# Perceiver layer on one core: the key stack's transfers on three queues and in the attention's block, routing in fewer and wider steps, own rows gathered tile by tile

## The reference, cut to what matters

```
x = x + cross_attention(layernorm(x), ctx)
Q, K, V = split(h @ WQ.T), split(h @ WK.T), split(h @ WV.T)     # h = layernorm(x)
Q, K = layernorm(Q), layernorm(K)                               # per head
context = softmax(Q @ K.T / sqrt(32)) @ V
z = context @ mean(sparse_W_V); z = z where z is among its head's 128 largest, else 0
x = x + (z * mean(sparse_W_O)) @ WO.T
probs = softmax(h2 @ Wg)                                        # h2 = layernorm(x), 8 experts
top_vals, top_idx = top_k(probs, 2); top_vals /= sum(top_vals)
x = x + sum over e of scores[e] * (relu(h2 @ W1[e] + b1[e]) @ W2[e] + b2[e])
```

## Time and profile before

| | us |
|---|---|
| median of 3 runs | 1640.94 (1640.29 to 1644.56) |
| the profiled execution | 1640.97 |
| its span, first to last instruction | 1639.3 |
| TensorE busy | 1523.3 |
| VectorE busy | 1265.9 |
| ScalarE busy | 1012.3 |
| GpSimd busy | 416.9 |

### The profile page before, as it was taken

The page is one execution under the profiler, slowest core; times in us unless marked ns, Lnnn a source line. Parts: engine busy times, 40 slices in busy tenths (PEclk is TensorE's granted clock), DMA queues, the critical chain, the costliest instruction groups (busy, mean ns, idle before and its releaser), DMA issues. The chain is left out here.

```text
span 1639.3 us, 22322 instructions
## 1 busy us (share of the span) xinstructions
PE 1523.3 (93%) x8112; PEld 836.7 (51%) x8112; DVE 1265.9 (77%) x1909; ACT 1012.3 (62%) x1241; POOL 416.9 (25%) x219
## 2 busy tenths in 40 slices
PE   6799999999999989999999999999877964799998
PEld 4466666666665433333333333333334421699996
DVE  5677676776777879999999999999665758477664
ACT  3366666666666678888888888888243530144441
POOL 5445545636545013204002100100104140100002
PEclk9899999999999989999999999999897986799999
DMA  4454444453534564456554445444342026289994
GB/s 171 162 190 145 167 168 149 160 180 129 193 142 142 140 156 126 112 150 187 126 143 114 123 110 128 115 117 103 52 99 56 1 97 269 72 308 355 365 351 135
DMA packets 119836, 254.50 MB, mean 155 GB/s; under 512 B 10152, under 2 KB 26536, under 8 KB 115248
## 3 DMA queue, kind: packets, MB, share of 16 engines
q1 hardware_dynamic: 118016, 248.88, 48.7%
q0 software_dynamic: 1280, 4.20, 0.8%
q10 hardware_dynamic: 432, 0.01, 0.0%
HBM read 182.26 MB, written 61.34 MB: 149 GB/s over the span
## 5 line engine op out<-in xcount | busy, mean ns | idle before, releaser
L748 ACT ACTIVATE att_pr<-att_sc 128x1024 f32<-128x1024 f32 x512 | 496.2, 1022 | 74.4 <-PE att_sc L665 74.4
L798 DVE TENSOR_TENSOR att_tot<-att_tot,att_pr 128x2048 f32<-128x2048 f32 x200 | 467.2, 2336 | 21.1 <-ACT att_pr L748 0.9
L491 DVE CUSTOM_DVE_ANT_0 ctx_size<-ctx_tot,ctx_size 128x512 f32<-128x512 f32 x512 | 333.1, 689 | 136.2 <-PE ctx_tot L411 132.1
L462 ACT ACTIVATE ctx_size<-ctx_dif 128x1024 f32<-128x1024 f32 x256 | 262.3, 1025 | 125.5 <-PE ctx_dif L411 125.4
L665 PE MATMUL att_sc<-g_stacks,att_kst 98*128 98x512 f32 x1024 | 308.8, 424 | 1.5 <-DVE g_stacks L589 1.5
L665 PEld LDWEIGHTS att_sc<-g_stacks,att_kst 98*128 98x128 f32 x1024 | 173.6, 189 | 236.1 <-ACT att_pr L748 210.8
L679 PE MATMUL att_o<-att_pr,att_val 128*32 128x512 f32 x2048 | 272.9, 605 | 2.0 <-issue 1.9
L411 PE MATMUL ctx_dif<-ctx_k_dif,f_q_hi 32*128 32x512 f32 x512 | 128.8, 500 | 8.9 <-DVE ctx_best L491 4.9
L411 PE MATMUL ctx_tot<-ctx_k_sum,f_q_hi 32*128 32x512 f32 x512 | 129.0, 500 | 0.0
L86 PE MATMUL f_proj<-f_wv_hi,g_stacks 128*128 128x512 f32 x320 | 121.1, 421 | 0.0
L86 PE MATMUL f_proj<-g_stacks,f_wk_hi 128*128 128x512 f32 x352 | 120.4, 424 | 0.0
(11 more groups left out here) (287 smaller groups left out, 2095.4 us busy)
## 6 DMA issues: line engine op xcount, KB each, us to landing
m_w<-in_W SPq DMA_DIRECT2D x30, 2048.0 KB, 10.6
att_kst<-keys_scratch SPq DMA_DIRECT2D x192, 256.0 KB, 3.9
f_raw<-in_ctx SPq DMA_DIRECT2D x32, 1024.0 KB, 6.0
keys_scratch<-f_k_hi SPq DMA_DIRECT2D x32, 512.0 KB, 2.8
keys_scratch<-f_k_lo SPq DMA_DIRECT2D x32, 512.0 KB, 3.2
values_scratch<-ctx_v SPq DMA_DIRECT2D x32, 512.0 KB, 3.1
att_val<-values_scratch SPq DMA_DIRECT2D x64, 256.0 KB, 2.7
rows_scratch<-mix_blank SPq DMA_DIRECT2D x1, 3840.0 KB, 23.7
```

Source lines behind the costliest of these rows:

```text
L462: act.activation(size[:, i % ABS, :], dif[:, :], ACT.Abs).then_inc(s_size, 1)
L491: dve.tensor_tensor_reduce(out=size[:, i % ABS, r * CH:(r + 1) * CH], in0=tot[i % 2][:, r * CH:(r + 1) * CH], in1=size[:, i % ABS, r * CH: ...
L748: act.activation(pr[:, T % SLOTS, 2 * s:2 * s + 2, :], sc[(2 * T + s) % PAIRS][:, :].rearrange("p (j q) -> p j q", j=2), ACT.Exp, scale=SC ...
L798: dve.tensor_tensor(tot[b % 2][:, :, :], so_far, pr[:, T % SLOTS, :, :], ALU.add).then_inc(s_add, 1)
```

## The change

**Key stack.** `key_rows` becomes a function that takes the issuing engine. In `self_projections` SyncE issues the high band at place 0 for group 0, ScalarE the one at place 2 (ahead of its last value copy), and GpSimd the low band (after `s_lo` has reached 8, with a semaphore of its own, `c.s_copy[2]`). The bands of groups 1 to 3 are issued by SyncE as its only work in `self_attend`. TensorE waits there for `c.s_copy[0]` and `c.s_copy[2]` before step 0, and for `c.s_copy[1]` before step 16 as before.

```diff
+def key_rows(engine, c, part, place, groups, done):
+    for j in range(HG):
+        src, dst = part[HD * j:HD * j + HD, groups, :], c.skst[HD * place:HD * place + HD, j::HG, :][:, groups, :]
+        engine.dma_start(f32(dst), src).then_inc(done, 16)
...
-            for groups, done in ((slice(0, 1), c.s_copy[0]), (slice(1, G), c.s_copy[1])):
-                sp.wait_ge(s_hi, TILES)
-                key_rows(f32(hi[1][:, :, :]), 0, groups, done)
-                key_rows(f32(hi[1][:, :, :]), 2, groups, done)
-                sp.wait_ge(s_lo, TILES)
-                key_rows(f32(lo[1]), 1, groups, done)
+            sp.wait_ge(s_hi, TILES)
+            key_rows(sp, c, f32(hi[1][:, :, :]), 0, slice(0, 1), c.s_copy[0])
...
             affine(TILES - 1)
+            act.wait_ge(s_hi, TILES)
+            key_rows(act, c, f32(hi[1][:, :, :]), 2, slice(0, 1), c.s_copy[0])
...
             pool.wait_ge(s_ones, 1)
+            pool.wait_ge(s_lo, TILES)
+            key_rows(pool, c, f32(lo[1]), 1, slice(0, 1), c.s_copy[2])
...
+        @block.sync
+        def _(sp):
+            for part, place in ((f32(c.own_hi[1][:, :, :]), 0), (f32(c.own_hi[1][:, :, :]), 2), (f32(c.own_lo[1]), 1)):
+                key_rows(sp, c, part, place, slice(1, G), c.s_copy[1])
...
-            pe.wait_ge(c.s_copy[0], 16 * HG * 6)
+            pe.wait_ge(c.s_copy[0], 16 * HG * 5)
+            pe.wait_ge(c.s_copy[2], 16 * HG)
```

```diff
-            for t in range(NT):
-                pe.matmul(count, every[:, :], mask[:, t, :], start=(t == 0), stop=(t == NT - 1)).then_inc(s_rank, 1)
-            for t in range(NT):
-                for u in range(t):
-                    pe.matmul(rank[:, t, :], every[:, :], mask[:, u, :], start=(u == 0), stop=False)
-                mm = pe.matmul(rank[:, t, :], earlier[:, :], mask[:, t, :], start=(t == 0), stop=True)
-            mm.then_inc(s_rank, 1)
+            for u in range(NT):
+                pe.matmul(rank[:, u + 1:, :], every[:, :], mask[:, 0:NT - u, :],
+                               start=(u == 0), stop=False, skip_group_check=True)
+            pe.matmul(rank[:, 0:NT, :], earlier[:, :], mask[:, :, :],
+                      start=False, stop=True, skip_group_check=True).then_inc(s_rank, 1)
...
+            tops = [go(dve.max(out=top[:, t, :], in_=prob[:, t, :])) for t in range(NT)]
             for t in range(NT):
-                step(dve.max(out=top[:, t, :], in_=prob[:, t, :]))
-                step(dve.max_index(out=idx[:, t, :], in_max=top[:, t, :], in_values=prob[:, t, :]))
...
+                dve.wait_ge(s_step, tops[t])
+                indexed = go(dve.max_index(out=idx[:, t, :], in_max=top[:, t, :], in_values=prob[:, t, :]))
+            summed = go(dve.tensor_tensor(two[:, :], top[:, :, 0], top[:, :, 1], ALU.add))
+            dve.wait_ge(s_step, indexed)
+            cast = go(dve.tensor_copy(idf[:, :, :], idx[:, :, :]))
+            dve.wait_ge(s_step, summed)
+            inverted = go(dve.reciprocal(rt[:, :], two[:, :]))
+            dve.wait_ge(s_set, 8)
+            dve.wait_ge(s_step, cast)
+            step(dve.tensor_tensor(pick[:, :, :, :], both(tall(iota[:, :])),
+                                   pairs(idf).unsqueeze(3).broadcast_to([P, 2, NT, E]), ALU.is_equal))
...
+            step(dve.tensor_tensor(more[:, :, :], count.unsqueeze(1).broadcast_to([P, 3, E]), edges[:, :, :], ALU.is_gt))
+            reached = go(dve.tensor_tensor(reach[:, :, :, :], more[:, :, :].unsqueeze(1).broadcast_to([P, E, 3, E]),
+                                           below[:, :, :, :], ALU.mult))
+            tiles = go(dve.tensor_reduce(extra[:, :], more[:, :, :].rearrange("p k e -> p e k"), AX.X, ALU.add))
+            dve.wait_ge(s_step, reached)
+            led = go(dve.tensor_reduce(ahead[:, :], reach[:, :, :, :].rearrange("p e k f -> p e (k f)"), AX.X, ALU.add))
...
+            step(dve.tensor_tensor(spots[:, :, :, :], pick[:, :, :, :], both(place[:, :, :]), ALU.mult))
+            step(dve.tensor_reduce(c.where[:, :, :], spots[:, :, :, :], AX.X, ALU.add))
+            dve.tensor_copy(c.slot[:, :].rearrange("p (k t) -> p k t", k=2), c.where[:, :, :]).then_inc(s_slot, 1)
```

```diff
+        OWN = (3, 5, 7, 8)
...
-                pe.wait_ge(s_own, 2 * NT)
-                for k in range(DC):
-                    for t in range(NT):
+                biases(range(0, NT // 2))
+                for t in range(NT):
+                    pe.wait_ge(s_own, OWN[t])
+                    for k in range(DC):
                         mm = pe.matmul(tx[:, k, :], c.h[:, t, k * P:(k + 1) * P], own[:, t, :],
-                                       start=(t == 0), stop=(t == NT - 1))
+                                       start=(t == k == 0), stop=(t == NT - 1), skip_group_check=True)
                 mm.then_inc(s_tx, 1)
...
+                biases(range(NT // 2, NT))
```

More of the change, by code:

```diff
@@ L937, in _ @@
         def _(sp):
-            def key_rows(part, place, groups, done):
-                for j in range(HG):
-                    src, dst = part[HD * j:HD * j + HD, groups, :], c.skst[HD * place:HD * place + HD, j::HG, :][:, groups, :]
-                    sp.dma_start(f32(dst), src).then_inc(done, 16)
             sp.wait_ge(s_hi, NT)
@@ L1369, in mix_and_route @@
         idf = sb("idf", [P, NT, 8])
-        pick = [sb(f"pick{k}", [P, NT, E]) for k in range(2)]
+        pick = sb("pick", [P, 2, NT, E])
         mask = sb("mask", [P, NT, E])
@@ L1374, in mix_and_route @@
         rt = sb("rt", [P, NT])
-        more = [sb(f"more{k}", [P, E]) for k in range(3)]
-        upto = [sb(f"upto{k}", [P, E]) for k in range(2)]
+        more = sb("more", [P, 3, E])
+        extra = sb("extra", [P, E])
+        reach = sb("reach", [P, E, 3, E])
+        ahead = sb("ahead", [P, E])
         move = sb("move", [P, E])
@@ L1621, in _ @@
-            step(dve.tensor_tensor(place[:, :, :], rank[:, :, :], late[:, :, :], ALU.add))
-            step(dve.scalar_tensor_tensor(out=place[:, :, :], in0=tall(iota[:, :]), scalar=128.0, in1=place[:, :, :],
-                                          op0=ALU.mult, op1=ALU.add))
-            for k in range(2):
-                step(dve.tensor_tensor(mine[:, :, :], pick[k][:, :, :], place[:, :, :], ALU.mult))
-                step(dve.tensor_reduce(c.where[:, k, :], mine[:, :, :], AX.X, ALU.add))
-                dve.tensor_copy(c.slot[:, NT * k:NT * k + NT], c.where[:, k, :]).then_inc(s_slot, 1)
@@ new lines, in _ @@
+            placed = go(dve.scalar_tensor_tensor(out=place[:, :, :], in0=tall(iota[:, :]), scalar=128.0, in1=rank[:, 0:NT, :],
+                                                 op0=ALU.mult, op1=ALU.add))
+            dve.wait_ge(s_step, led)
+            moved = go(dve.scalar_tensor_tensor(out=move[:, :], in0=ahead[:, :], scalar=128.0, in1=shifted[:, :],
+                                                op0=ALU.mult, op1=ALU.add))
+            dve.wait_ge(s_step, tiles)
+            go(dve.tensor_tensor(c.upto[:, :], ahead[:, :], extra[:, :], ALU.add))
@@ new lines, in _ @@
+            dve.wait_ge(s_step, moved)
+            step(dve.scalar_tensor_tensor(out=late[:, :, :], in0=rank[:, 0:NT, :], scalar=128.0, in1=tall(move[:, :]),
+                                          op0=ALU.is_ge, op1=ALU.mult))
+            dve.wait_ge(s_step, placed)
+            step(dve.tensor_tensor(place[:, :, :], place[:, :, :], late[:, :, :], ALU.add))
+            step(dve.tensor_tensor(spots[:, :, :, :], pick[:, :, :, :], both(place[:, :, :]), ALU.mult))
+            step(dve.tensor_reduce(c.where[:, :, :], spots[:, :, :, :], AX.X, ALU.add))
@@ L1645, in _ @@
                       allow_small_or_imprecise_dtypes=True).then_inc(s_set, 1)
-            pool.wait_ge(s_set, 4)
+            pool.wait_ge(s_set, 6)
+            pool.affine_select(out=below[:, :, :, :].rearrange("p e k f -> p e (k f)"),
+                               in_=every[:, 0:3 * E].unsqueeze(1).broadcast_to([P, E, 3 * E]),
+                               compare_op=ALU.is_gt, fill=0.0, base=0, pattern=[[1, E], [0, 3], [-1, E]],
+                               channel_multiplier=0).then_inc(s_set, 1)
             pool.affine_select(out=earlier[:, :], in_=every[:, :], compare_op=ALU.is_gt, fill=0.0,
@@ L2010, in perceiver_layer @@
                 c.own_lo = [c.own_pr[:, n, :, :] for n in range(2)]
-                c.s_copy = [sem(f"copy{n}") for n in range(2)]
+                c.s_copy = [sem(f"copy{n}") for n in range(3)]
                 self_projections(nc, c)
```

108 lines of the change are left out of this document (55 added, 53 removed).

## The result

The kernel after took 1628.51 us (median of 4 runs, 1626.45 to 1632.10), the kernel before 1642.15 beside it (1640.29 to 1644.56): ratio 0.9918, 95% interval 0.9895 to 0.9941, so 13 us gained, 10 to 17. The forecast was 1624.9. The profiled execution of after is its longest, 1632.10 (span 1630.4), against 1640.97 of before: 8.9 us less.

What follows compares the result with a forecast made beforehand. TensorE, 93% busy, was taken as the bound on average, idling at the key stack and routing. Parts of 9.0, 5.0 and 2.1 sum to 16.1: 1640.97 to 1624.9 us; own range 1622 to 1628, with rivals 1 and 2 1620 to 1632.

Steps and rivals of the forecast that it cites:

- What bounds the kernel: Whole kernel: TensorE bounds on average, 93% busy; an 18.2 us gap without compute and the routing's VectorE chain delay it.
- Part A: Key stack: issues spread over three engines, groups 1 to 3 moved; TensorE restarts at 1228.5 instead of 1237.55, 9.0 us gained.
- The barrier's own term: Between projections and attention: TensorE's first product follows the last issue by 0.94 us, so 1227.6, before the landing at 1228.5.
- Rivals 1 and 4: GpSimd's key transfers: 1, dear at 2.2 us each, 1628.7, chance 0.18; 4, they hold the core, 1646 at 6.5, chance 0.03.
- rival 3: Attention: starts early but is held at product 17 by the transfers of groups 1 to 3; about 1641, chance 0.03.
- Same cost as now: Attention's restart: the clock falls in the shorter gap and rises some 4 us after work begins, as before; no loss taken.
- rival 2: Clock pattern differs: low stretch at 1256 to 1262 goes (1622) or costs (1628), or biases don't lift it (1626.6); chance 0.24.
- Part B: Routing: fewer operations, no waits between independent ones, five wide counting products instead of 14 narrow; 5.0 us gained.
- Part C: Head of the experts: two biases first, then own rows by tile at the full clock; first expert product 2.1 us sooner.
- so it rises at O + 3.9: Head of the experts: clock up 3.9 us after O, the opening of the experts' block, so own rows run at full clock.
- Rival 2's clause: Head of the experts: if 8-row biases do not bring up the clock, own rows end at O + 9.4, 0.35 us gained.
- The next constraint: Experts: tile 1's rows land at O + 15.6, wanted at O + 16.7; cover of 1.1 us, late next.

Runs made afterwards that it cites:

- e5: The kernel after with group 0's low band of key rows issued by SyncE instead of GpSimd; 1625.95 us, ratio to before 0.9917.
- e12: e10 with 6 unread products behind the last self-projection transposes and 2 at the head of the attention's block; 1622.51 us, ratio to before 0.9900.
- e10: e9 with unread products in the routing's waits (three and two) and the biases' operands zero-filled to 128 rows; 1623.34 us, ratio to before 0.9906.
- e6: The kernel after with the two new small tiles placed in an old tile, restoring the experts' tile addresses; 1628.34 us, ratio to before 0.9929.
- e4: The kernel after with all four biases behind the own rows; 1628.12 us, ratio to before 0.9912.
- e7: e4 with five unread products on TensorE in the routing, three before the mask wait and two behind the scores' transposes; 1625.69 us, ratio to before 0.9918.
- e3: The kernel before with only own rows by tile and the split biases and comparisons; 1639.62 us, ratio to before 0.9988.
- e8: The kernel after with six unread products on TensorE behind key products 10 to 15 of the attention's lead; 1628.39 us, ratio to before 0.9935.
- e1: The kernel before with the key stack's part alone; 1633.17 us, ratio to before 0.9945.
- e2: The kernel before with the routing's part alone, the owner's steps moved too; 1640.10 us, ratio to before 0.9990.
- e9: The kernel after with the edits of e4, e5 and e6 together; 1625.76 us, ratio to before 0.9920.

## Why the prediction was right, and where it was not

- **What bounds the kernel** held in the main: the tail followed the restart and the first expert product, less what the clock and the addresses took back. (That no engine computes for 18.2 us is too much: ScalarE and VectorE still work in the first 2.3 us of it.) From the mark on, after is 10.3 us shorter in the profile: gap -8.84, attention +2.14, routing -5.24, head +0.17, experts +1.56, the rest -0.13.
- **Part A, 9.0: the size held (8.84), by errors that cancel.** GpSimd's issues were taken at 1.24 and 1.26 us each from its indirect ones; plain ones cost 0.50 to 0.77, 2.30 for four instead of 5.0, and begin 0.66 after the split that they wait for. The landing was put 1.77 us after the last issue, from indirect ones too; it came 3.39 after it, and TensorE starts 0.74 behind it, for which nothing was counted. That the landing decides held, but by a way that the prediction did not have: TensorE waited for the block, and the block for GpSimd. The barrier's own term, 0.94 after the last issue, was wrong for GpSimd (4.13) and right for SyncE (e5: 0.65 to the opening). Rivals 1 and 4 fall with the issue price; rival 3 falls since there is no wait at product 17.
- **"Same cost as now" for the clock failed.** Attention and next took 167.1 us instead of 165.1 in the profile, and 166.5 to 167.5 in the eight profiles with the short gap: 1.4 to 2.5 us given back. In after the low clock lasts 6.4 us of the restart instead of 4.1 (the first transposes of the maxima 1.3 us later) and 10.3 in the second stretch instead of 6.8 (the rest 0.9 longer). That is rival 2's kind, at both places. Why the stretches are as long as they are stays open: with the same short gap the first one is 3.1 to 6.4. Nor is it shown that a high clock at the restart gets the 2 us back: e12 has it and takes 163.7, but e10 takes 164.3 without it.
- **Part B, 5.0: right at its place (5.24), and so in its working**: unwaited operations at 0.11, five wide products as cheap per record as narrow ones (2.35 us from the counting's start to VectorE's release, forecast 2.3). By the Trainium skill's "VectorE: DVE Perf Modes", The DRAIN you can't avoid, the prediction's estimate for this part was 3.6; the row decides against it for these sizes. The Trainium skill, "VectorE: DVE Perf Modes", Two Vector instructions with no wait between them, has only a held operation wait until every earlier one has finished, and the 0.11 agrees with that: it is less than the 0.19 that the operation before it takes. What the step missed is outside it: its two new tiles shifted the experts' and cost 1.6 us there (e6).
- **Part C, 2.1: failed, -0.17.** The step that failed is "so it rises at O + 3.9": TensorE was busy from O on, with biases of 8 rows first, and the clock rose at O + 8.3. Rival 2's clause (0.35 gained) came closer. With the rows first, e4 gains 1.25 on before; e7, which also keeps TensorE busy in the routing, 3.2; e10, with padded biases too, 3.5.
- **The next constraint was named right**: tile 1's rows, expected at O + 15.6, were there by O + 15.3 in e10 and came at O + 16.7 in e12, when the head was short enough to meet them.
- **The sum**, 16.1, is 13.4 [9.7, 17.2] by time and 10.3 in the profile. The three costs that were not foreseen (2.1, 2.3 short in part C, 1.6) make 6.0, about the profile's shortfall. The measured 1628.51 is outside the prediction's own range of 1622 to 1628 and beside rival 1's 1628.7, which is luck: dear issues did not happen. It is inside the range with both rivals because the clock's costs are of rival 2's kind; the 1.6 us of the addresses stand in no rival.

## What to carry to other kernels

Ask of every edit ahead of TensorE what clock it restarts at, and put products on all rows of the array first at such a place; filling short ones up with zeros cost no time here (1.88 us against 1.98). After an edit that adds a tile, compare the mean of untouched instruction groups downstream; memory layout is part of the change. When GpSimd issues transfers as its last act in a block, look for the next block's opening at their landing and not at their issue. And before a microsecond in one stage of one profile is put down to an edit, look at the same stage in profiles that share its instructions: here it moved by 1.4 to 1.6 us by itself.

## What the runs showed of the hardware

- Products on 8 rows kept TensorE busy for 3.75 us without raising the clock (after; e3, e5, e6 and e8 alike). A run of 3.7 us of them at 2.4 GHz was followed by 3.4 us at 1.2 (e7), and e1 and e2 had such a stretch too, but before, e4 and e9 did not; on 128 rows none followed (e10 to e12). The Trainium skill, "TensorE: Matmul & The Clock Gate", What's actually happening, says that the clock follows how busy the array has been recently; the trace of after agrees only in part, as TensorE was busy on 8 rows and the clock stayed at 0.50.
- With GpSimd's transfers last, a block ended 3.79 to 3.85 us behind the end of its last issue and 0.45 to 0.46 behind its landing (six profiles); with SyncE's, 0.65 behind the issue, with transfers still under way (e5).
- A plain transfer of 64 KB cost GpSimd 0.50 to 0.77 us to issue (after), SyncE 0.56 to 0.60.
- 64 bytes of address cost 3 to 4 ns on a product record of 390 to 402 (e6).
